# One meeting of the engines between two stages instead of two, and TensorE turns the identity while it waits in the heads of three stages

## What is computed

```python
x = x + _L0_xattn_ref(_layernorm(x), ctx_1024, w_q, b_q, w_kv, b_kv, w_out, b_out)
x = x + _L0_ffn_ref(_layernorm(x), centroids, Wp, bp, W1, b1, W2, b2)
x = x + _L1_xattn_ref(_layernorm(x), ctx_1024, Wq, Wkv, Wout, mask)
x = x + _L1_ffn_ref(_layernorm(x), w1, conv_w, conv_b, w2)
...
# L0 ffn: 8 experts (256 -> 1024 -> 256, gelu), the 2 nearest centroids per token
top_v, top_i = jax.lax.top_k(routing_logits, TOP_K)
out = jnp.einsum('bne,bned->bnd', comb, y)
...
# L1 ffn: up with rounded weights, a convolution over the tokens, silu, down
h = bit_linear(x, w1); h = depthwise_conv1d(...); h = silu(h); out = bit_linear(h, w2)
```

## Time and profile before

| | |
|---|---|
| time, median of 3 runs | 641.51 us (639.17 to 641.65) |
| profiled execution: time, span | 639.72 us, 638.0 us |
| mean granted clock of TensorE | 0.946 |
| busy: PE, DVE, ACT, POOL | 541.9, 364.3, 364.4, 179.3 us |
| first instruction behind the seams (DVE) | 2.32, 204.43, 388.44, 579.25 us |
| end of the output's last issue | 634.73 us |

### The profile page before, as it was taken

One profiled execution on the slowest core, in us unless ns is written; L12 is line 12 of the kernel. 1 busy time (PEld: TensorE's weight loads), 2 busy tenths in 40 slices (PEclk: granted clock), 3 DMA queues, 4 the chain that ended last, 5 costly groups with the idle time before them and its releaser, 6 DMA issues. The chain is left out here.

```text
span 638.0 us, 14767 instructions
## 1 busy us (share of the span) xinstructions
PE 541.9 (85%) x5314; PEld 463.2 (73%) x5314; DVE 364.3 (57%) x1129; ACT 364.4 (57%) x863; POOL 179.3 (28%) x274
## 2 busy tenths in 40 slices
PE   3898999999885269999999996789989999865746
PEld 2777878888763159999999996677878888754535
DVE  3776675666754701131322114689687787855895
ACT  2778888778754023322333223478888888743654
POOL 2132453434314151111211004702343343433000
PEclk9999999999998569999999998779999999987998
DMA  6472102112002987757555504311101110000002
GB/s 163 140 204 76 52 24 73 51 50 73 7 1 60 359 322 259 248 186 223 192 179 177 199 16 110 114 58 49 51 4 48 51 49 3 2 2 0 1 1 58
DMA packets 33530, 62.80 MB, mean 98 GB/s; under 512 B 4162, under 2 KB 24467, under 8 KB 33332
## 3 DMA queue, kind: packets, MB, share of 16 engines
q1 hardware_dynamic: 29716, 47.97, 23.0%
q0 software_dynamic: 2928, 10.75, 5.9%
q10 hardware_dynamic: 816, 3.15, 1.3%
HBM read 51.11 MB, written 10.75 MB: 97 GB/s over the span
## 5 line engine op out<-in xcount | busy, mean ns | idle before, releaser
L1562 ACT ACTIVATE ex_h_t<-ex_h,b_e 128x128 f32<-128x128 f32 x168 | 48.0, 368 | 125.4 <-PE ex_h L1746 125.4
L1153 PEld LDWEIGHTS a_ring<-ident,w_all 112*125 112x125 f32 x768 | 91.2, 193 | 23.8 <-issue 13.0
L1153 PE MATMUL a_ring<-ident,w_all 112*125 112x112 f32 x768 | 102.8, 285 | 6.5 <-ACT w_all L613 6.5
L621 ACT ACTIVATE w_all<-a_ring 125x448 f32<-125x448 f32 x128 | 63.1, 542 | 46.8 <-PE a_ring L1153 46.7
L1746 PE MATMUL ex_h<-ex_xg_t,w_s 128*128 128x128 f32 x672 | 80.3, 279 | 0.3 <-issue 0.3
L1746 PEld LDWEIGHTS ex_h<-ex_xg_t,w_s 128*128 128x128 f32 x672 | 78.6, 196 | 0.5 <-issue 0.5
L856 DVE TENSOR_REDUCE a_mx<-a_s 112x2 f32<-112x750 f32 x64 | 59.6, 931 | 28.9 <-PE a_s L1144 28.9
L1765 PE MATMUL ex_y<-w_all,ex_h_t 128*128 x336 | 75.9, 379 | 0.0
L863 DVE CUSTOM_DVE_ANT_0 w_all<-a_s,mask_sb 112x375 f32<-112x375 f32 x128 | 65.4, 544 | 18.3 <-PE a_ring L36 10.9
L613 ACT ACTIVATE w_all<-w_all,a_shift 112x375 f32<-112x375 f32 x128 | 69.7, 601 | 6.7 <-DVE a_shift L868 5.0
L1668 DVE TENSOR_TENSOR ex_y_sb<-ex_y,b_all 128x256 f32<-128x256 f32 x21 | 8.9, 425 | 104.6 <-PE ex_y L1765 104.4
(11 more groups left out here) (297 smaller groups left out, 808.3 us busy)
## 6 DMA issues: line engine op xcount, KB each, us to landing
w_s<-in_L_ffn_W SPq DMA_DIRECT2D x18, 1024.0 KB, 5.4
w_all<-in_L_ffn_W SPq DMA_DIRECT2D x8, 1024.0 KB, 11.7
ct_dram<-a_ct SPq DMA_DIRECT2D x8, 752.0 KB, 4.4
a_ct<-ct_dram POOLq DMA_DIRECT2D x8, 752.0 KB
w_s<-in_L_ffn_W ACTq DMA_DIRECT2D x3, 1024.0 KB, 11.3
w_all<-in_ctx SPq DMA_DIRECT2D x8, 375.0 KB
y_slots<-ex_y_sb SPq DMA_DIRECT2D x21, 128.0 KB, 1.7
w_ud<-in_L_ffn_w SPq DMA_DIRECT2D x2, 1024.0 KB, 9.4
```

Source lines behind the costliest of these rows:

```text
L621: a.activation(et[:, t % 2, kc], bank("et", t, kc)[0:KP, 0:4 * S], ACT.Copy)\
L1153: last = nc.tensor.transpose(bank("et", t, kc)[0:KP, r * S:(r + 1) * S], es[:, t % 2, r, kc * KP:(kc + 1) * KP], ident[0:S, 0:S])
L1562: last = a.activation(h_t[:, i % 2, f], hb[i % 2][:, f * 128:(f + 1) * 128], ACT.Gelu, bias=b1_e[:, i % 2, f:f + 1])
```

## The change

`end_phase` no longer clears semaphores or makes the engines meet. A new function `begin_phase` is called just ahead of each block, when the stage's own semaphores have been allocated: it clears those of the stage before, on GpSimd, with no meeting behind it. The first attention, the experts and the second attention get a function `keep_busy(bank, n)` on TensorE: n transposes of the identity into a PSUM bank that nothing reads before it is written again.

```diff
+    past_sems = []
...
+    def begin_phase():
+        if past_sems:
+            nc.clear_and_free_semaphores(list(past_sems))
+        past_sems.clear()
+        past_sems.extend(phase_sems)
+        phase_sems.clear()
+
     def end_phase():
-
-        nc.clear_and_free_semaphores(list(phase_sems))
-        phase_sems.clear()
-        nc.all_engine_barrier()
         scope.pop()
...
+        def keep_busy(bank, n):
+
+            for _ in range(n):
+                nc.tensor.transpose(bank[:, 0:128], ident[:], ident[:])
...
+                begin_phase()
                 with nc.Block() as block:
...
                         if first:
+                            keep_busy(s, 30)
                             context(0, 0)
                             context(0, 1)
+                            keep_busy(s, 4)
                             biases()
...
                             for q in range(3, 8):
                                 ffn_weight(q)
+                            keep_busy(s, 16)
                             turned_x(0, 0)
                             turned_x(0, 1)
+                            keep_busy(s, 8)
                         wait_weight(1, 0)
                         queries(0, 0)
...
                         pe.wait_ge(source_out, 1)
+                        keep_busy(hb[1], 26)
                         turn(0)
```

## The result

The changed kernel takes 638.77 us (median of 20 runs, 636.96 to 642.55) against 641.67 for the one before (20 runs, 637.17 to 646.3). The ratio is 0.9956, with a 95% interval of 0.9935 to 0.9977: 2.8 us, between 1.5 and 4.2, where 5.6 had been forecast. The time lies at the very edge of the range of the prediction (631.5 to 638.8). Measured again later, on two chips, the ratio was 0.9981 (0.9964 to 0.9998) and 0.9991 (0.997 to 1.0013), which is 1.2 and 0.6 us. The time lies where the first rival put it, 638.5: the filling brought nothing. That it comes so near is in part luck, since the repeats show less than the rival's 3.0 us. The profiled execution takes 639.39 us, 0.3 less than that of before.

The account below looks back on a forecast made before the run. Bound at the stage seams by double engine meetings and TensorE's half-clock starts behind them: 3.0 us from meetings plus 2.6 from filling, 5.6 off 639.72, gives 634.1, median put at 635; range 631.5 to 638.8.

Parts of the forecast that it names:

- the first rival: Fillers do not help: clock does not rise by them or falls in the gap; 638.5 us on the median, chance 0.22.
- What the filling gives: Faster TensorE work at the start of three heads through a higher clock: sum 2.6 us, bounds 0 and 6.0.
- Filling, first head: First attention: faster first products and L1118, bounds 0 to 1.9 us, 0.8 taken; clock may fall before 10 us.
- Filling, second head: Experts: faster first expert products and turns, bounds 0 to 2.1 us, 0.6 taken; fillers end 1.8 to 3 us early.
- Filling, third head: Second attention: queries at full clock, bounds 0 to 2.0 us, 1.2 taken; filling free or 0.2 late.
- the idle 2.92 us shrinks to 1.0: Second attention: 16 fillers from 401.6 to 403.5 us cut TensorE's wait for `xn` before 404.54 us.
- Second meeting: Seam before the experts, 203.3 us: VectorE's routing chain and the weight loads start 1.0 us earlier, gain 1.0.
- First meeting: Start of the first attention, 1.8 us: SyncE's loads leave 0.4 us earlier, gain 0.4.
- Third: Seam before the second attention, 387.7 us: GpSimd still clears before issuing loads; -0.2 to +0.3 us, 0 taken.
- Fourth: Seam before the last stage, 578.1 us: TensorE starts at once behind the release, gain 1.0 us, or 0.7.
- End: Last meeting, at 637.4 us: nothing follows it, gain 0.6 us.
- The rule on transposes: Skill's rule that transposes do not count for the clock; would leave 3.0 us alone. Prediction went by the rows instead.

Follow-up runs that it names:

- e10: Changed kernel with only the first head filled, and longer (62, 8 and 4 turned identities): 638.86 us, ratio 0.9974 to the kernel before.
- e12: Changed kernel with longer filling in the first two heads, 8 fillers behind the third head's turning of x, 16 in the last stage: 635.57 us, ratio 0.9938.
- e16: The program of e12 measured again, beside the kernel before, single meetings alone and the changed kernel: 633.44 us, ratio 0.9894.
- e5: Changed kernel with longer filling reaching to the real work in the first two heads, none in the third: 634.61 us, ratio 0.9888.
- e4: Changed kernel without the third head's filling, keeping the first two heads' 30, 4 and 26: 636.24 us, ratio 0.995 to the kernel before.
- e9: The changed kernel itself, measured again: 639.09 us, ratio 0.9981 to the kernel before.
- e1: Changed kernel with all five fillings removed, single meetings alone: 638.28 us, ratio 0.9975 to the kernel before.
- e3: Changed kernel with only the third head's filling (16 and 8) kept: 636.89 us, ratio 0.9964 to the kernel before.
- e11: Changed kernel with only the experts' head filled, and longer (54 and 8 turned identities): 637.61 us, ratio 0.9956 to the kernel before.
- e15: The changed kernel itself, measured once more beside single meetings alone: 639.23 us, ratio 0.9991 to the kernel before.
- e8: Single meetings, filling in the third head alone, with 48 fillers in place of 16 ahead of the turning of x: 643.46 us, ratio 1.0028.
- e2: The filling alone: changed kernel with the two meetings and the clear between them put back: 639.52 us, ratio 1.0012 to the kernel before.
- e13: The kernel before, measured again as a measure of itself: 639.3 us, ratio 0.9992.
- e14: Single meetings alone, the program of e1 measured again: 636.32 us, ratio 0.9947 to the kernel before.
- e7: Single meetings without filling, 5 MB of the experts' weight loads held until the first gather has landed: 642.83 us, ratio 1.0012.

## Why the prediction was wrong

That TensorE starts at half clock behind each seam was read rightly, and so was the doubt that the clock can fall in a gap. What failed is the weight given to that doubt: the sum of "What the filling gives", 2.6 us, measured nothing. The terms in order:

- **Filling, first head: "I take 0.8".** Nothing. The prediction named the doubt ("the clock can fall again before 10 us") and still took half of the bound. The gap was 3.52 us and the fall came at 12.4. With the gap closed the first scores come 0.9 to 1.6 us earlier than in the changed kernel measured beside them (e10, e12, e16), and in e5 1.9 earlier than in after: from half of the bound to all of it.
- **Filling, second head: "I take 0.6".** Nothing on the real work, and a price that was not foreseen: in the five runs with 26 fillers the first turn stands 7.8 to 8.0 us after the cast, in the eight with none and the loads unchanged 7.4 to 7.5. The gather lands later. In the DMA view of 219 to 230 us a transfer of instructions on queue q8, 0.02 MB, stands in after, e4 and e9, and none in before, e1 and e3; but e5 has it too with the turn at 7.6 us, so that it delays the gather is not shown. The bound of this head, 2.1, was too low: with the gap closed the first down-projection came 2.2 to 2.4 us earlier than in the changed kernel beside it (e11, e12, e16).
- **Filling, third head: "I take 1.2", cost "free or 0.2 late".** Net nothing, in two ways. In the profile after and in e9 the fillers stood late before ready work: queries 2.0 us faster, turning 1.8 later. In e15 they stood as forecast, and the clock fell all the same in the 2.7 us behind them. In e3 1.99 us were left, the clock held, and the scores came 1.0 us earlier than in e1: near the 1.2, once. The step that failed is "the idle 2.92 us shrinks to 1.0": it took the slack between two engines from one trace, and it measured 0 in two executions of the changed kernel and 2.7 in the third. e8 bears out the prediction's warning that a filling whose cover is gone is paid in full.
- **Second meeting: "1.0".** VectorE's chain did start 1.2 us earlier than before, 1.0 of it by the meeting. Three rows of before, then the same three of after:

```profile
206.49 0.42 DVE L1586 TENSOR_SCALAR rt_den<-rt_den 112x64 f32<-112x64 f32 x1
208.60 0.20 DVE L1590 TENSOR_SCALAR rt_a<-rt_a 112x64 f32<-112x64 f32 x1
208.82 0.22 DVE L1595 TENSOR_REDUCE rt_pair<-rt_a 112x8 f32<-112x64 f32 x1
```

```profile
205.15 0.35 DVE L1605 TENSOR_SCALAR rt_den<-rt_den 112x64 f32<-112x64 f32 x1
206.98 1.08 DVE L1609 TENSOR_SCALAR rt_a<-rt_a 112x64 f32<-112x64 f32 x1
208.09 0.22 DVE L1614 TENSOR_REDUCE rt_pair<-rt_a 112x8 f32<-112x64 f32 x1
```

  The lead shrinks from 1.34 to 0.73 us by the third row shown; the second takes 1.08 us in place of 0.20. That repeats: this operation takes 1.07 to 1.09 us in all fifteen profiles of kernels with single meetings and 0.20 us in the three with two (before, e2, e13). GpSimd, which clears the semaphores first, starts its constants at 204.19 against 204.39 before, so they now lie beside a later part of VectorE's chain. "GpSimd's constants lie beside that chain" was taken as free and cost 0.6. That it is GpSimd's work beside it which slows VectorE is argued from the times. Then the later gather took 0.4, and the first down-projection stands 36.4 us after the first release, as before. Of 1.0, nothing came through in the changed kernel.
- **First meeting: "0.4".** SyncE's loads leave earlier, the context is turned at 10.67 against the 10.48 of the earlier trace rows. In the other runs it starts at 10.1 to 10.7 with the change's filling and at 10.4 to 11.2 where no filling stands ahead, a scatter larger than 0.4 us. Not to be seen.
- **Third: "0".** `xn` ends 16.8 us after the release, before and after; right. **Fourth: "1.0".** Without the fall in that stage 0.4 to 1.2 (stage 4: 58.5 to 58.7 against 59.1 to 59.7 in before, e2 and e13), in the changed kernel nothing: TensorE came 1.4 us earlier, and the clock fell at 585.8 instead of 589.3. **End: "0.6".** 0.6, since nothing follows.
- **The rule on transposes.** The grant rose at 5.6 and 224.0 us, at 4.6 and 223.1 when repeated, with nothing but turned identities running. The Trainium skill, TensorE: Matmul & The Clock Gate, Part 4: PE-mode transpose, says that transposes do not count; these runs disagree. The first rival's time came true by the second of its two reasons, the fall in the gap, and not by that rule.

What the 2.8 us of the changed kernel consist of can't be resolved: 0.6 stands at the end, the rest lies within the scatter of the stages, and the repeats of the whole gave 1.2 and 0.6. The ratios say that the meetings alone are worth 1.6 us (0.9975, with an interval that reaches past 1) and 3.4 us (0.9947), about the 3.0 that the prediction gave them, and that the filling added to them gives nothing; that it takes some of it back is what e14 and e15 show side by side, once.

## What to carry to other kernels

Filling that raises the clock pays if it reaches to the real work. Here, in the first two heads, fillings that ended 1.8 to 3.5 us too early lost the clock in all five profiles that had them and paid nothing; fillings without a gap kept it in seven heads of eight and brought the first scores or the first down-projection 0.9 to 2.5 us forward, of which up to 2.4 us and sometimes nothing was left at the stage's end. Beyond the cover a filler is paid one for one. So size it by the time at which its successor becomes ready, at the full-clock price of a filler, and place it where that time is set by a transfer and not by an engine whose lead changes from run to run. A barrier's time counts only where the first thing behind it isn't waiting for the engine that does the clearing, or for transfers that move at their own pace: follow the lead from mark to mark, not only from the release.

## What the runs showed of the hardware

- The grant rose with identity transposes alone, as above. It fell after an idle stretch, within it, or without one. In the changed kernel's first profile work resumed at 10.67 and 228.58 us, the grant fell at 12.4 and 230.8 and stayed at 0.50 for 6.8 and 3.4 us, with TensorE busy 6.23 of 6.80 and 3.40 of 3.40 us. In e15 it fell at 9.9 and 405.8 us, before work resumed at 10.13 and 406.49. In e16 it fell at 15.4 us with no idle stretch over 0.45 us since the filling began.
- One of VectorE's small operations on 112x64 values takes 0.20 us in before and 1.08 us where it lies beside GpSimd's casts, in every profile with single meetings.
- From the cast of `source` to the first turn of the gathered rows 7.4 us pass beside the full weight transfers (e1) and 4.3 us with part of them held back (e7).
- In the third head of some executions ScalarE or VectorE stand idle 2 to 5 us for a result of TensorE whose matmuls had ended. ScalarE in the changed kernel's first profile:

```profile
400.96 0.87 ACT L592 ACTIVATE w_all<-a_ring 125x512 f32<-125x512 f32 x2 [4.65 <-remote]
```

  TensorE's matmuls of those values end by 398.0 (395.74 and 2.23). All profiles of e5 to e8 and of e9 to e12 have such waits, none of e1 to e4 and of e13 to e16 has, the same program now with and now without. What holds the signal back stays open.
